# Keys and values made in an earlier stage: a four-layer attention and expert kernel

## The reference

```python
x = x + xattn_n(layernorm(x), ctx, ctx, Wq, bq, Wk, bk, Wv, bv, Wo, bo)
x = x + ffn_n(layernorm(x), ...)

def xattn(query, key, value, ...):       # 16 heads of 8 features
    q = query @ Wq.T + bq
    k = key @ Wk.T + bk                  # key and value are the context,
    v = value @ Wv.T + bv                # the same in all four layers
    ...                                  # layer 0 causal, layer 2 masked,
    a = softmax(q k^T (scaled))          # layer 3 turns q and k by position
    return (a v) @ Wo.T + bo
```

## Time and profile before

| what | us |
|---|---|
| median of 3 runs | 1567.35 |
| lowest and highest | 1565.18, 1569.91 |
| the profiled execution | 1563.71 |
| its span, first to last instruction | 1561.7 |

### The profile page before, as it was taken

One profiled execution on the slowest core, in us unless ns is written; L12 is line 12 of the kernel. 1 busy time (PEld: TensorE's weight loads), 2 busy tenths in 40 slices (PEclk: granted clock), 3 DMA queues, 4 the chain that ended last, 5 costly groups with the idle time before them and its releaser, 6 DMA issues. The chain is left out here.

```text
span 1561.7 us, 38528 instructions
## 1 busy us (share of the span) xinstructions
PE 1235.4 (79%) x13615; PEld 805.7 (52%) x13624; DVE 924.1 (59%) x2265; ACT 615.8 (39%) x1476; POOL 553.1 (35%) x1109
## 2 busy tenths in 40 slices
PE   3999987998999971699379999966699987755640
PEld 2566655665566661477245565644356655433420
DVE  6577755556678854244473555538668867393325
ACT  1266552222366641355222444431046655432210
POOL 2145512001155412503331343201635513646860
PEclk9899995999799975799787999978889997985555
DMA  5000002700000040212100000010000002232329
GB/s 187 1 4 3 3 32 72 230 1 1 1 2 3 3 176 14 76 54 82 44 1 1 2 3 2 3 56 1 0 2 2 3 6 62 81 136 48 52 35 269
DMA packets 84300, 68.45 MB, mean 44 GB/s; under 512 B 10608, under 2 KB 80048, under 8 KB 82992
## 3 DMA queue, kind: packets, MB, share of 16 engines
q1 hardware_dynamic: 75952, 56.88, 11.7%
q0 software_dynamic: 8192, 9.45, 3.2%
HBM read 42.00 MB, written 24.30 MB: 42 GB/s over the span
## 5 line engine op out<-in xcount | busy, mean ns | idle before, releaser
L483 DVE TENSOR_REDUCE a_m<-psum 128x4 f32<-128x512 f32 x512 | 329.5, 685 | 218.9 <-PE psum L386 92.7
L525 ACT ACTIVATE a_pt<-psum 128x512 f32<-128x512 f32 x512 | 294.4, 601 | 267.5 <-PE psum L414 267.5
L370 PE MATMUL psum<-h_kbd,h_qT 32*128 32x512 f32 x1024 | 322.3, 679 | 23.9 <-PEq L184 21.6
L379 PE MATMUL psum<-h_qbd,h_kT 32*128 32x512 f32 x1024 | 306.8, 654 | 0.0
L570 POOL CAST max_parts<-a_m 128x16 bf16<-128x16 f32 x128 | 25.1, 196 | 365.4 <-DVE a_m L483 365.4
L423 PE MATMUL psum<-a_pt,v_x 128*32 128x128 f32 x4096 | 138.8, 276 | 1.0 <-ACT a_at L553 1.0
L370 PEld LDWEIGHTS psum<-h_kbd,h_qT 32*128 32x128 f32 x1024 | 91.8, 193 | 77.1 <-issue 47.7
L414 PEld LDWEIGHTS psum<-a_mt,minus_sb 32*128 32x128 bf16 x2048 | 86.5, 94 | 84.7 <-issue 70.1
L423 PEld LDWEIGHTS psum<-a_pt,v_x 128*32 128x32 f32 x4096 | 104.4, 110 | 14.7 <-issue 1.8
L414 PE MATMUL psum<-a_mt,minus_sb 32*128 32x128 bf16 x2048 | 109.3, 216 | 0.0
L379 PEld LDWEIGHTS psum<-h_qbd,h_kT 32*128 32x128 f32 x1024 | 86.5, 187 | 2.8 <-issue 1.6
(11 more groups left out here) (262 smaller groups left out, 2626.4 us busy)
## 6 DMA issues: line engine op xcount, KB each, us to landing
sum_rows<-zero_row SPq DMA_DIRECT2D x1, 8320.0 KB, 36.7
end_sums<-sum_rows SPq DMA_DIRECT2D x16, 512.0 KB, 7.3
w_w<-in_f_w SPq DMA_DIRECT2D x2, 2048.0 KB, 9.9
w_up<-in_f_up SPq DMA_DIRECT2D x1, 4096.0 KB
slots_x<-zero_row SPq DMA_DIRECT2D x2, 1536.0 KB, 10.1
e_xb<-slots_x SPq DMA_DIRECT2D x48, 64.0 KB, 1.8
slots_y<-e_y SPq DMA_DIRECT2D x48, 64.0 KB
x_sb<-in_x SPq DMA_DIRECT2D x4, 512.0 KB, 6.0
```

The lines of the kernel that those rows point to most:

```text
L370: return nc.tensor.matmul(score_bank[job % 3], c.qT[r, tokens(t)], c.kbd[r, t // GT % 2, :, within(t)], start=True, stop=not masked)
L379: nc.tensor.matmul(turned_bank[job % 3], c.kT[r, tokens(t)], c.qbd[r, t // GT % 2, :, within(t)], start=True, stop=False)
L483: nc.vector.reduce_max(m[:, t % 2, 4 * r:4 * r + 4], score_bank[job % 3].rearrange("p (h k) -> p h k", h=4), AX).then_inc(maxed, 1)
L525: nc.scalar.activation(pt[:, t % 2, 4 * r:4 * r + 4, :].rearrange("p h q -> p (h q)"), turned_bank[job % 3], ACT.Exp, scale=scale).then_in ...
```

## The change

Keys and values of a layer are made in the feed-forward part before it (those of layer 0 in `setup`), by new functions that put one group's work on each engine: `context_tensor` (key matmul, in layer 3 also that with the permuted weight, four value matmuls), `context_scalar` (both moved out of PSUM by ACT, the key's bias added) and, for layer 3, `context_gpsimd` (two products with cosine and sine and their sum on Pool). They stand

- in `setup`, as soon as half of the context is there; the context, one layer's weights and the biases are now loaded ahead of `x`, and the masks and the other layers' weights behind all else,
- in `route` of layer 0: two groups ahead of the transposes, six behind the logits,
- in `routed_gelu`: all eight ahead of the experts,
- in `ffn2`: one group ahead and one behind each expert's first two matmuls.

`project` keeps the queries. PE now works one group behind with them: it transposes group i, then makes the queries of group i - 1. Pool spreads the first keys at once; the Exp table is loaded at the start of ACT's work. Queries lie in the buffer that held the values. The values' bias no longer goes to the values: softmax rows sum to one, so `bv @ Wo.T` is added to the output bias, for layer 0 in `setup`, for layers 1 to 3 at the end of project 0, where the masks are now also converted.

The shared expert of layer 3 is no longer split: all of it is in `dispatch`, and turned. The tokens are the moving side in its first matmuls, four tiles at once (16 jobs: 8 groups by 2 halves of the inner width), so its product needs no transposition. Its stream on PE starts when DVE has read the selection.

The diff, cut to its core:

```diff
+def context_tensor(nc, c, s, pe, g):
+
+    src = c.ctxT[:, g * GN:(g + 1) * GN]
+    k_bank, v_bank = s.k_bank[g % len(s.k_bank)], s.v_bank[g % len(s.v_bank)]
+    if g >= len(s.k_bank):
+        pe.wait_ge(s.k_kept, g + 1 - len(s.k_bank))
+    last = nc.tensor.matmul(k_bank, s.wk, src, start=True, stop=True)
+    if s.rope:
+        last = nc.tensor.matmul(s.other_bank[g % len(s.other_bank)], c.wrot[:, 1, :], src, start=True, stop=True)
+    last.then_inc(s.k_psum, 1)
+    if g >= len(s.v_bank):
+        pe.wait_ge(s.v_kept, g + 1 - len(s.v_bank))
+    for j in range(GT):
+        last = nc.tensor.matmul(v_bank[:, j * P:(j + 1) * P], src[:, j * P:(j + 1) * P], s.wv, start=True, stop=True)
+    last.then_inc(s.v_psum, 1)
...
+def context_scalar(nc, c, s, act, g):
+
+    k_bank, v_bank = s.k_bank[g % len(s.k_bank)], s.v_bank[g % len(s.v_bank)]
+    bias = c.bcol[:, 2 * s.layer + 1:2 * s.layer + 2]
+    act.wait_ge(s.k_psum, g + 1)
+    if s.rope:
+        if g >= 2:
+            act.wait_ge(s.k_ready, 3 * (g - 1))
+        nc.scalar.activation(s.rot[:, g % 2, 0, :], k_bank, ACT.Identity, bias=bias)
+        nc.scalar.activation(s.rot[:, g % 2, 1, :], s.other_bank[g % len(s.other_bank)], ACT.Identity,
+                             bias=c.bcol[:, 9:10]).then_inc(s.k_kept, 1)
+    else:
+        nc.scalar.activation(c.kT[:, g * GN:(g + 1) * GN], k_bank, ACT.Identity, bias=bias).then_inc(s.k_kept, 1)
+    act.wait_ge(s.v_psum, g + 1)
+    nc.scalar.activation(c.vk[:, g * GT:(g + 1) * GT, :].rearrange("p j f -> p (j f)"), v_bank,
+                         ACT.Identity).then_inc(s.v_kept, 1)
...
+def context_gpsimd(nc, c, s, pool, g):
+
+    pool.wait_ge(s.k_kept, g + 1)
+    for n in range(2):
+        half = s.rot[:, g % 2, n, :].rearrange("p (j t) -> p j t", j=GT)
+        nc.gpsimd.tensor_tensor(half, half, c.rope[:, n:n + 1, :].to_broadcast([P, GT, P]), ALU.mult).then_inc(s.k_ready, 1)
+    pool.wait_ge(s.k_ready, 3 * g + 2)
+    nc.gpsimd.tensor_tensor(c.kT[:, g * GN:(g + 1) * GN], s.rot[:, g % 2, 0, :], s.rot[:, g % 2, 1, :],
+                            ALU.add).then_inc(s.k_ready, 1)
...
-    c.qT, c.kT, c.qbd, c.kbd = scratch(nc, own, f"h{layer}", dict(
+    c.qT = c.v.rearrange("p t f -> p (t f)")
+    c.qbd, c.kbd = scratch(nc, own, f"h{layer}", dict(qbd=([P, 2, 4, GN], F32), kbd=([P, 2, 4, GN], F32)))
...
-            def keys(g):
-                dve.wait_ge(k_psum, g + 1)
-                nc.vector.tensor_scalar(c.kT[:, cols(g)], k_bank[g % 2], bias[1], None, ALU.add).then_inc(k_ready, 1)
-
-            def values(g):
-                dve.wait_ge(v_psum, g + 1)
-                nc.vector.tensor_tensor(
-                    c.v[:, g * GT:(g + 1) * GT, :], v_bank[g % 2].rearrange("p (j f) -> p j f", j=GT),
-                    c.brow[:, 2 * layer:2 * layer + 1, :].to_broadcast([P, GT, P]), ALU.add).then_inc(v_ready, 1)
...
+            if layer == 0:
+                dve.wait_ge(c.late_in, 16 * c.late_loads)
+                for n in range(3):
+                    last = nc.vector.tensor_copy(wide[:, n, :], c.bcol[:, 11 + n:12 + n].to_broadcast([P, P]))
+                last.then_inc(bv_wide, 1)
+                convert_masks(nc, c)
+                dve.wait_ge(bv_psum, 1)
+                nc.vector.tensor_tensor(c.brow[:, 1:4, :], c.brow[:, 1:4, :],
+                                        bv_bank[:, 0:3 * P].rearrange("p (n f) -> p n f", n=3), ALU.add)
...
+            load_table(nc, c, ACT.Exp)
...
+            for g in range(2):
+                expand(c.kbd, c.kT, g)
+            for g in range(NG if rope else 2):
                 if rope:
-                    combine(g, 1)
-                    combine(g, 0)
-                if not rope and g in (1, 2):
-                    expand(g - 1)
-            if rope:
-                expand(0)
-                expand(1)
+                    combine(g)
+                if g < 2:
+                    pool.wait_ge(q_ready, g + 1)
+                    expand(c.qbd, c.qT, g).then_inc(expanded, 1)
...
+            for i in range(NG + 1):
+                if i < NG:
+                    pe.wait_ge(xn_ready, i + 1)
+                    if i >= 2:
+                        pe.wait_ge(xt_ready, i - 1)
+                    for j in range(GT):
+                        last = nc.tensor.transpose(xt_bank[i % 2][:, j * P:(j + 1) * P], xn[:, i % 2, j, :], c.ident[:])
+                    last.then_inc(xt_psum, 1)
+                g = i - 1
+                if g >= 0:
+                    pe.wait_ge(xt_ready, g + 1)
+                    if g >= 2:
+                        pe.wait_ge(turned if rope else q_ready, g - 1)
+                    last = nc.tensor.matmul(q_bank[g % 2], wq, xnT[:, g % 2, :], start=True, stop=True)
+                    if rope:
+                        last = nc.tensor.matmul(other_bank[g % 2], c.wrot[:, 0, :], xnT[:, g % 2, :], start=True, stop=True)
+                    last.then_inc(q_psum, 1)
...
-                project_into(k_bank, g, wk, 1, c.ctxT[:, cols(g)], turned if rope else k_ready, k_psum)
-                if g >= 2:
-                    pe.wait_ge(v_ready, g - 1)
-                for j in range(GT):
-                    last = nc.tensor.matmul(v_bank[g % 2][:, j * P:(j + 1) * P], c.ctxT[:, tokens(g * GT + j)], wv,
+                pe.wait_ge(bv_wide, 1)
+                for n in range(3):
+                    last = nc.tensor.matmul(bv_bank[:, n * P:(n + 1) * P], wide[:, n, :], c.wa[:, n + 1, 3, :],
                                             start=True, stop=True)
-                last.then_inc(v_psum, 1)
...
+    for n in range(s.JOBS + s.LAG):
+        if n < s.JOBS:
+            g, k = n // 2, n % 2
+            src = c.xT[:, g * GN:(g + 1) * GN]
+            if n >= 2:
+                pe.wait_ge(s.gu_ready, n - 1)
+            nc.tensor.matmul(s.gate_bank[n % 2], s.w["up"][:, k * P:(k + 1) * P], src, start=True, stop=True)
+            nc.tensor.matmul(s.up_bank[n % 2], s.w["up"][:, (2 + k) * P:(3 + k) * P], src,
+                             start=True, stop=True).then_inc(s.up_psum, 1)
+        m = n - s.LAG
+        if m >= 0:
+            g, k = m // 2, m % 2
+            pe.wait_ge(s.h_ready, m + 1)
+            if k == 0 and g >= 2:
+                pe.wait_ge(s.yg_ready, g - 1)
+            for j in range(GT):
+                last = nc.tensor.matmul(s.y_bank[g % 2][:, j * P:(j + 1) * P], s.h[:, m % 3, j * P:(j + 1) * P],
+                                        s.w["down"][:, k, :], start=k == 0 and j == 0, stop=k == 1 and j == GT - 1)
...
+            if layer == 0:
+                for g in range(2):
+                    context_scalar(nc, c, keys, act, g)
...
             load_table(nc, c, ACT.Gelu if layer == 1 else ACT.Silu)
+            if layer == 0:
+                for g in range(2, NG):
+                    context_scalar(nc, c, keys, act, g)
             if big:
                 act.wait_ge(gate_ready, 1)
-                shared_scalar(nc, c, shared, act)
...
+            if layer == 0:
+                for g in range(2):
+                    context_tensor(nc, c, keys, pe, g)
             pe.wait_ge(gate_in, 16)
...
             run_steps(pe, step, 2, 2, NG // 2 - 1, NG + 1)
-            if big:
-                pe.wait_ge(loaded, 16 * (len(loads) - 1))
-                shared_tensor(nc, c, shared, pe)
+            if layer == 0:
+                for g in range(2, NG):
+                    context_tensor(nc, c, keys, pe, g)
...
+            for g in range(NG):
+                context_tensor(nc, c, keys, pe, g)
+            pe.wait_ge(keys.k_kept, NG)
+            pe.wait_ge(keys.v_kept, NG)
...
+            for g in range(NG):
+                context_scalar(nc, c, keys, act, g)
...
+        keys = Context(nc, c, 3, own, ([c.bank[5]], [c.bank[6]], [c.bank[7]]))
+
+        @block.gpsimd
+        def _(pool):
+            for g in range(NG):
+                context_gpsimd(nc, c, keys, pool, g)
...
+            context_tensor(nc, c, keys, pe, 0)
...
+                if i + 1 < NG:
+                    context_tensor(nc, c, keys, pe, i + 1)
...
+            context_scalar(nc, c, keys, act, 0)
...
+                if e + 1 < NG:
+                    context_scalar(nc, c, keys, act, e + 1)
...
+            pe.wait_ge(sel_read, 1)
             shared_tensor(nc, c, shared, pe)
-            pe.wait_ge(sel_read, 1)
...
+        heads = [(c.wa[:, 0], d["wa"][:, 0]), (c.bcol[:], d["bcol"])]
+        loads = [(c.ident[:], d["ident"]), (c.head_of[:], d["head_of"]), (minus[:], d["minus"]),
+                 (before[:], d["before"]), (within[:], d["within"]), (c.brow[:], d["brow"].partition_broadcast(P))]
+        lates = [(c.wa[:, 1:4], d["wa"][:, 1:4]), (c.wrot[:], d["wrot"]), (c.rope[:], d["rope"]),
+                 (c.causal[:], d["causal"]), (c.ident_rows_in[:], d["ident_rows"]), (c.umask[:], d["umask"])]
...
+                for dst, src in heads:
+                    sp.dma_start(dst, src).then_inc(first, 16)
```

(64 more changed lines are left out.)

233 lines of the change are left out of this document (80 added, 153 removed).

## The result

The changed kernel takes 1542.03 us (median of 4 runs, 1540.22 to 1544.43) where the kernel before takes 1566.26 on the same chips: a ratio of 0.9847, interval 0.9822 to 0.9872. The forecast was 1507, the range 1485 to 1534. The kernel became faster, by 24 us where 59 were forecast.

What follows compares the result with a forecast made beforehand. No single engine was taken as the bound; each block was costed by what ends last in it, with two clock values for PE. Terms summed to -59 from 1563.7 (1504.7; 1508.3 by the median), forecast 1507 us, range 1485 to 1534.

Steps and rivals of the forecast that it cites:

- DVE: 1.9 + 15.2 + 8 x 1.48 = 28.9, then one combination and the barrier: 31.5.: Project 3: DVE's start, normalising and turns, then the end; block falls from 58.9 to 31.5 us, gain 27 (13 to 30).
- 45 in all: Project 3, low end of the gain: PE at half clock needs 4.3 us a group, 45 us in all.
- The first rival: Projects: clock stays low, costing 8.7 in each of 1 and 2, 13 in 3, 30 in all: 1537; chance 0.13.
- the prediction's own signs of being wrong: Prediction is wrong if the projects' granted clock is 0.5 to 0.7, or if the attentions' own lengths change.
- +14: Layer 2 experts: added context work, with three Pool operations a group, lengthens the block by 14 us (+7.6 to +17).
- So Pool sets the pace: Layer 2 experts: Pool's three operations, 4.0 us a group with waits, limit the block; seven groups end 7.6 later if unhindered.
- the lock: Layer 2 experts: DVE and Pool share a port; Pool slowed to 5.24 us a group would make the term +16.6.
- Its list of DVE's operations: Layer 2 experts: DVE operations with two SBUF operands, 0.41 + 0.41 + 0.61 us per expert, added to Pool's 3.8.
- Projects 0 to 2: Key and value work leaves these blocks: gains of 11.7 in project 0 and 11.1 each in projects 1 and 2.
- Layer 3 from its route on: Shared expert moved whole into dispatch: route 3 -17.1, dispatch +3, forecast -14.1 us together.
- 17 + 4.1: Project 0: DVE's 17 us plus its tail of masks, copies and bias sum, written as 21.0; gain 11.7.
- the chances of the cases: Whole kernel: forecast as summed 0.48; the rivals 0.13, 0.12, 0.08, 0.16 and, for slower than before, 0.02.

Runs made afterwards that it cites:

- e4: Changed kernel with layer 3's keys left unturned, so no Pool work in the layer 2 experts' block: block 47.4 us, kernel 1538.28 us (one execution).
- e6: Changed kernel with DVE two groups ahead in project 3, three context groups ahead of the layer 2 experts' weights, keys turned by DVE: 1511.90 us, ratio 0.9636.

## Why the prediction was wrong

**Project 3: the step that failed.** "DVE: 1.9 + 15.2 + 8 x 1.48 = 28.9, then one combination and the barrier: 31.5." The sum takes DVE as never waiting. Its terms were nearly right (DVE's busy time is 30.00), but in the changed order DVE and PE wait for each other once in every group, and a group costs the sum of both. The block is 10.9 us up to the first turn (1071.38), six groups of 7.4 to 8.3 up to the seventh turn (1118.85), together 47.5, and 4.6 behind it. Even the worst case, "45 in all" with PE at half clock, is one engine's work alone. The ring stands in the diff: it could have been read from the order of the instructions before any run. Cutting it at either place (36.1 and 40.8 us) shows it.

The first rival's claim that the clock would fall in the projects came true in this block (0.65, one of the prediction's own signs of being wrong), but as a consequence: with the clock raised, 51.3 remained.

With the ring cut on DVE's side, 4.6 us above the forecast are left. DVE begins its tiles 3.5 us into the block instead of 1.9: Pool now spreads the keys there, and beside it the layer norm's small operations take 0.58 to 0.64 us (0.19 in the kernel before). DVE then waits 2.7 for the first queries. And every four tiles take 2.05 us beside a sum of Pool's and 2.4 to 2.8 where an expansion runs, too; the prediction has 1.10 for half of them.

**The layer 2 experts: a mis-sized term.** +14 was forecast, +19.8 came. "So Pool sets the pace" is the step that failed: PE and DVE set it. Without any Pool work 11.8 remain (e4): PE's 3.92 per expert and its first matmuls at half clock, a sum that the prediction didn't make. The other 8.0 go with Pool's work, and most of that is DVE's delay: the prediction saw the lock and charged it to Pool, but DVE paid. Its list of DVE's operations left out the clipping, which was stretched most. So +14 came from a wrong path, and that it is not further off is luck. How much of the 8.0 is the lock alone stays open: e6 moves two of three Pool operations away and gains 3.9.

Which engine pays could be read before. In project 3 of the kernel before, Pool's combination stands beside DVE's tiles, not only beside the turns:

```profile
1088.38 2.05 DVE L201 TENSOR_SCALAR p_xn<-x_sb,mean_var,ln_rstd 128x128 f32<-128x128 f32 x4
...
1088.54 1.30 POOL L277 TENSOR_TENSOR h_qT<-p_rot 128x512 f32<-128x512 f32 x1 [0.64 <-DVE p_rot L225]
```

Pool keeps its 1.3 and DVE's four tiles take 2.05 instead of 1.10. The prediction took the unchanged 1.29 as a sign that there is no conflict.

The page "SBUF — State Buffer" of the Trainium skill, on the shared port pair, says that the loser of the lock stands still for the whole instruction. The trace agrees: one clipping of 0.29 us took 1.36 (from 1022.63) and ended at 1023.99, 0.15 behind two Pool products that had begun before it (1021.09 to 1023.84). In this kernel the loser was mostly DVE.

**What was right.** Projects 0 to 2 fell by 10.0, 10.5 and 11.0 where 11.7, 11.1 and 11.1 were forecast. Project 1's clock was 0.73 in the mean, low at first, as the sum had it. The page "TensorE: Matmul & The Clock Gate" of the Trainium skill, Part 1, has a busy engine rise to the high clock. The trace agrees within project 1 and, as soon as the ring is cut, in project 3; it doesn't in the first route, where PE is busy for 34.89 of 36.70 us at a clock of 0.72 (before: 20.14 of 20.30 at 0.50). Layer 3 from its route on gave 15.1 where 14.1 were forecast; the dispatch took 56.9 us, near 57 as said. Feed-forward 0 cost 4.8 instead of 3; the experts of layer 1 hid their eight groups wholly; setup cost 1.1 instead of gaining 0.5.

Of the 35.7 us by which the span missed the sum, 31.1 are project 3's and 5.8 the layer 2 experts', the attentions gave 6.6 back, and 5.4 are left for all other terms. That the attentions gave and didn't take is luck: their work is the same (last section).

Three slips of the prediction changed nothing: 17 + 4.1 is 21.1, not 21.0; the earlier trace rows show 1.29 for a Pool operation, not 1.27; and the chances of the cases add up to 0.99, so 0.01 was left for mishaps, not 0.02.

## What to carry to other kernels

A block that is fed by two engines in turn isn't costed by its busiest engine alone: write down, for one step, what stands ahead of each instruction in its own queue, and look for a ring. If software pipelining delays one engine by a group, the other must run a group further ahead, or the two orders close. When work is moved into another block, add it up on each engine there, also on the one that looked idle, and ask which engine loses when two share a port.
